# Group 3's reads: summed over d by a 0/1 matrix in two parts, then one float32 product with the outgoing weights

## What is computed

```python
x = layernorm(x + L0_attn(x))      # gated linear recurrence, 16 heads of 8
x = layernorm(x + x @ W[idx] + b[idx])   # one of 8 experts, chosen from logits and noise
x = layernorm(x + L1_attn(x))      # linear attention through a metric, 16 heads of 8
x = layernorm(x + L1_ffn(x))       # 128 -> 512 gated, 512 -> 512 gelu, twice, 512 -> 128
```

```python
k = sigmoid(x @ key_w.T + key_b)                 # [n, t, head, d]
upd = (1 - k)[..., :, None] * v[..., None, :]    # d x e per head
kv[t] = kv[t-1] * k[t] + upd[t]                  # a scan over t
h[e] = sum over d of q[d] * kv[d, e]
out = h @ out_w.T + out_b
```

## Time and profile before

| | us |
|---|---|
| median of 3 runs (193.44 to 194.26) | 193.96 |
| the profiled execution's own time | 193.92 |
| its span, first to last instruction | 192.1 |
| busy PE | 173.9 |
| busy DVE | 143.7 |
| busy ACT | 124.9 |
| busy POOL | 69.6 |

### The profile page before, as it was taken

How to read it: one execution, slowest core, us unless ns; L and a number is a source line. 1 busy time by engine, 2 the same in 40 slices (tenths; PEclk the granted TensorE clock), 3 DMA queues, 4 the chain that set the end, 5 groups by cost and what they waited for, 6 DMA issues and landing times. The chain is left out here.

```text
span 192.1 us, 2885 instructions
## 1 busy us (share of the span) xinstructions
PE 173.9 (91%) x949; PEld 138.1 (72%) x949; DVE 143.7 (75%) x371; ACT 124.9 (65%) x207; POOL 69.6 (36%) x65
## 2 busy tenths in 40 slices
PE   7779796999999999999999999999899999999930
PEld 7447483768977788888888899876678775586810
DVE  0799999999999997679979986668470774804461
ACT  3895915963838588648786560577887578975720
POOL 1020002640330662525172740442556336285320
PEclk9999999999999999999999999999999999999985
DMA  4879400210000001000000000000001000010102
GB/s 116 257 198 430 181 2 22 68 48 0 3 0 0 5 22 32 0 0 3 0 0 2 3 0 0 0 0 3 0 3 55 5 0 0 0 54 1 55 7 58
DMA packets 6705, 7.85 MB, mean 41 GB/s; under 512 B 544, under 2 KB 5664, under 8 KB 6432
## 3 DMA queue, kind: packets, MB, share of 16 engines
q1 hardware_dynamic: 6688, 7.63, 12.2%
HBM read 6.58 MB, written 1.05 MB: 40 GB/s over the span
## 5 line engine op out<-in xcount | busy, mean ns | idle before, releaser
L878 DVE TENSOR_TENSOR_SCAN state<-rep_bank,keep 128x256 f32<-128x256 f32 x62 | 38.6, 672 | 0.0
L347 POOL TENSOR_TENSOR rstd<-varied,power 128x4 f32<-128x4 f32 x15 | 15.9, 1063 | 57.0 <-DVE varied L937 57.0
L1335 PEld LDWEIGHTS y_bank<-attend_pack,read 128*128 128x128 f32 x256 | 31.4, 192 | 4.5 <-issue 2.6
L1335 PE MATMUL y_bank<-attend_pack,read 128*128 128x128 f32 x256 | 32.8, 276 | 0.7 <-DVE read L888 0.3
L585 ACT ACTIVATE hid_even_high<-c_bank,scales_pack 128x512 fp32r<-128x512 f32 x15 | 10.3, 689 | 17.9 <-PE c_bank L1430 17.9
L356 POOL TENSOR_TENSOR hid_odd_low<-hid,hid_odd_high 128x512 fp32r<-128x512 f32 x12 | 15.9, 1323 | 15.2 <-ACT hid L591 15.1
L591 ACT ACTIVATE hid<-c_bank,scales_pack 128x512 f32<-128x512 f32 x31 | 21.2, 684 | 0.0
L888 DVE TENSOR_TENSOR read<-state,query 128x512 f32<-128x512 f32 x28 | 20.8, 754 | 0.0
L1430 PE MATMUL c_bank<-hid_even_high,hidden_rounded 128*128 128x512 f32 x64 | 19.2, 411 | 0.5 <-ACT gate L574 0.5
L1430 PE MATMUL c_bank<-hid_odd_low,hidden_rounded 128*128 128x512 f32 x64 | 18.5, 398 | 0.5 <-DVE hid_odd_low L1033 0.5
L1430 PE MATMUL c_bank<-hid_even_low,hidden_rounded 128*128 128x512 f32 x64 | 18.7, 398 | 0.0
(11 more groups left out here) (189 smaller groups left out, 359.4 us busy)
## 6 DMA issues: line engine op xcount, KB each, us to landing
hidden_pack<-hidden SPq DMA_DIRECT2D x2, 1024.0 KB, 10.1
xt<-x_tok SPq DMA_DIRECT2D x4, 256.0 KB, 2.9
xT_lent<-x_chan SPq DMA_DIRECT2D x3, 256.0 KB, 4.6
mlp_pack<-mlp SPq DMA_DIRECT2D x1, 768.0 KB, 7.1
out<-xT_lent SPq DMA_DIRECT2D x3, 256.0 KB, 2.3
attend_pack<-attend SPq DMA_DIRECT2D x1, 640.0 KB, 4.2
metric_pack<-metric SPq DMA_DIRECT2D x1, 448.0 KB, 5.8
xT_lent<-x_chan SPq DMA_DIRECT2D x2, 128.0 KB, 2.5
```

The lines of the kernel that those rows point to most:

```text
L347: nc.gpsimd.tensor_tensor(rstd[n][:], varied[n][:], power[:], ALU.pow).then_inc(ln_rstd[n], 1)
L878: ins = nc.vector.tensor_tensor_scan(state[:, e % STATES, at], rep_bank[e % 2][:, at], keep[:, a * T + s * SEQ:a * T + (s + 1) * SEQ], 0.0 ...
L1335: ins = nc.tensor.matmul(y1_bank[:, tile(j)], read[:, e % READS, tile(j)], out_w_rep_sb[:, e, :], start=(e == 0 and j == 0), stop=False, s ...
```

## The change

For group 3 alone (`GATHERED = (3,)`) the eight `attend` calls go. In their place, for each `e`:

- `upper_read(3, e)` (ACT): copies `read` to `read_high`, rounded float32 (128x512, two buffers);
- `lower_read(3, e)` (DVE): `read - read_high` into `read_low`, which lies in the two buffers `dvalue_parts[0]` of the even groups' value steps;
- `gather(3, e)` (PE): two products of 512 columns, for the high and the low part, with a shifted window of a 0/1 matrix (`gather_r`) as weights. It sums over d and puts the 16 heads of index `e` on rows of their own in `y1_bank`.

After the last one `join(3)` (DVE) adds `direct` to `y1_bank` and writes `direct`, and `attend_joined(3)` (PE) multiplies that by `out_w` in four float32 products. `cast_gather` (ACT) rounds the matrix once; it comes in with the `metric` pack, which is 240 columns (120 KB) wider. The core of the diff:

```diff
+        gather_r = sb("gather_r", [P, GATHER], F32R)
+        read_high = sb("read_high", [P, 2, T], F32R)
+        read_low = dvalue_parts[0]
...
+            def upper_read(a, e):
+                act.wait_ge(*read_done(a, e))
+                if gathered(a, e) > 2:
+                    act.wait_ge(attended, HD * a + e - 1)
+                nc.scalar.copy(read_high[:, e % 2, :], read[:, e % READS, :]).then_inc(upper_done, 1)
...
+            def lower_read(a, e):
+                dve.wait_ge(upper_done, gathered(a, e))
+                if gathered(a, e) > 2:
+                    dve.wait_ge(attended, HD * a + e - 1)
+                nc.vector.tensor_tensor(read_low[e % 2][:], read[:, e % READS, :], read_high[:, e % 2, :].bitcast(F32),
+                                        ALU.subtract).then_inc(lower_done, 1)
+
+            def join(a):
+                dve.wait_ge(attended, HD * (a + 1))
+                dve.wait_ge(direct_ready, a + 1)
+                nc.vector.tensor_tensor(direct[a % 2][:], y1_bank[:], direct[a % 2][:], ALU.add).then_inc(joined, 1)
...
+            def gather(a, e):
+                if e == 0:
+                    pe.wait_ge(gather_cast, 1)
+                    pe.wait_ge(ln_sum[0], a)
+                    if a > 2:
+                        pe.wait_ge(ln_sum[3], a - 2)
+                at = (HD - 1 - e) * HEADS
+                pe.wait_ge(upper_done, gathered(a, e))
+                nc.tensor.matmul(y1_bank[:], gather_r[:, at:at + P], read_high[:, e % 2, :], start=(e == 0), stop=False)
+                pe.wait_ge(lower_done, gathered(a, e))
+                nc.tensor.matmul(y1_bank[:], gather_r[:, at:at + P], read_low[e % 2][:], start=False,
+                                 stop=(e == HD - 1)).then_inc(attended, 1)
+
+            def attend_joined(a):
+                pe.wait_ge(joined, GATHERED.index(a) + 1)
+                for j in range(NT):
+                    ins = nc.tensor.matmul(y1_bank[:, tile(j)], direct[a % 2][:, tile(j)], out_w_sb[:],
+                                           start=True, stop=True)
+                ins.then_inc(y1_ready, 1)
```

With this the lists of calls of PE, DVE, ACT and POOL are written anew nearly throughout, in all four groups; the other steps are the same ones, in another order. Of PE's list, for example:

```diff
+                hidden(0, 2, 3)
+                replicate(3, 4)
+                narrow(0)
                 transposes(1, 2)
-                hidden(0, 2, 2)
-                replicate(3, 2)
```

More of the change, by code:

```diff
@@ L755, in _ @@
             high_x3(3)
+            silu_table(3)
+            narrow_out(2)
             silu(3, 0)
-            narrow_out(2)
+            silu(3, 1)
             high_product(3, 0)
-            silu(3, 1)
             silu(3, 2)
@@ L1197, in _ @@
             norm_moments(2, 2)
+            norm_varied(2, 2)
+            join(3)
+            norm_out(2, 2)
+            low_gelu(1, 2, 2)
             norm_sum(0, 3)
-            norm_varied(2, 2)
+            low_gelu(1, 2, 3)
             norm_stats(0, 3)
             norm_moments(0, 3)
-            norm_out(2, 2)
             norm_varied(0, 3)
@@ L1650, in with_weights @@
-                hidden(0, 1, 2)
-                replicate(3, 0)
-                through_metric(1)
-                replicate(3, 1)
-                hidden(0, 1, 3)
-                metric_out(1)
                 attend(2, 6)
                 attend(2, 7)
+                attend_direct(2)
+                transposes(1, 1)
+                hidden(0, 1, 2)
+                heads_of(1)
+                hidden(0, 1, 3)
+                gram_of(1)
+                replicate(3, 2)
+                replicate(3, 3)
@@ L1658, in with_weights @@
+                mix(1)
                 hidden(0, 2, 0)
-                attend_direct(2)
+                through_metric(1)
                 hidden(0, 2, 1)
+                metric_out(1)
+                hidden(0, 2, 2)
+                hidden(0, 2, 3)
+                replicate(3, 4)
+                narrow(0)
                 transposes(1, 2)
-                hidden(0, 2, 2)
-                replicate(3, 2)
-                hidden(0, 2, 3)
-                replicate(3, 3)
+                replicate(3, 5)
@@ L1666, in with_weights @@
+                turn_back(0)
+                replicate(3, 6)
                 gate_of(1, 0)
+                transposes(2, 0)
                 up_of(1, 0)
-                narrow(0)
+                gate_of(1, 1)
+                routed(2)
                 up_of(1, 1)
-                transposes(2, 0)
-                replicate(3, 4)
-                gate_of(1, 1)
+                gate_of(1, 2)
+                gather(3, 0)
+                gate_of(1, 3)
                 up_of(1, 2)
-                turn_back(0)
@@ L1814 @@
         "blocks": blocks,
+        "gather": np.concatenate([np.zeros((P, P - HEADS)), blocks[:, ::HD], np.zeros((P, P - HEADS))], 1,
+                                 dtype=np.float32),
         "ident": np.eye(P, dtype=np.float32),
```

509 lines of the change are left out of this document (262 added, 247 removed).

## The result

| | before | after |
|---|---|---|
| median of 4 runs | 194.11 us | 197.05 us (196.73 to 197.3) |
| ratio, 95% interval | | 1.0163, 1.0127 to 1.02 |
| profiled execution, its span | 193.92, 192.1 | 196.82, 195.0 |

The account below looks back on a forecast made before the run. The start was taken as bound by DVE, PE as nearly gapless from the first gate to about 132 us. Saving -3.5, start -0.3, waits and 0.4 for POOL summed to +1.1: 195.0 us, range 192.0 to 197.4.

Parts of the forecast that it names:

- this mechanism: Main case: the new order's waits give back PE's saving and somewhat more, 193.5 to 196.3 us; chance 0.45.
- Saving: Group 3's sum on PE: eight gathers at 0.47 us instead of attends at 0.90, 3.5 us saved.
- The start: Up to the first gate product: DVE's list 0.5 us shorter, gate up to 0.5 us earlier, 0.3 taken.
- Item 2: After `hidden(0, 2, 3)` ends, at h: `replicate(3, 6)` needs a scan behind ACT and DVE; 1.3 us, bounds 0.3 and 2.
- Item 3: `product(1, 1)` behind `lower_read(3, 1)` and `norm_sum(1, 2)` moves `hidden(1, 1, 0)`: 1.0 us, bounds 0 and 1.5.
- the 0.4 which I had taken for the lock: Term for DVE steps held back by POOL at places without slack: 0.4 us added.
- Item 1: Blocks 2 and 3 of group 1 closer together, several waits between 58 and 92 us: 0.8, bounds 0 and 1.5.
- Item 4: `turn_back(1)` directly behind `narrow(1)` waits for ACT's `narrow_out`: 0.9 us, bounds 0.6 and 1.0.
- item 5: Group 2's gate stage: `norm_stats(1, 3)` makes `hidden(2, 1, 0)` late by 0.9; `metric_out(3)` waits 0.65; together 1.5 us.
- Item 6: Waits gone (0.31, 0.62, and 0.42 in group 3), 0.3 new before `hidden(3, 1, 0)`: net -1.0, bounds -1.35 and 0.
- DVE becomes the bound: Rival: POOL holds back subtractions and reads, group 3's sum 3 us later, 197 to 198; 0.12 together with the gathers' rival.
- the saving survives: Rival: items 1 to 3 and 5 near their lower bounds, sum -2.0, 191.9 us; chance 0.28.

Follow-up runs that it names:

- c_old_start: The changed kernel with the start of before (PE's list up to `attend(2, 2)`, DVE's up to `low_x3(0)`): 196.74 us, ratio 1.0112.
- i_best: The changed kernel's operations, lists of before up to 59 us, behind it some instructions of DVE, ACT and PE moved a few places: 192.76 us, ratio 0.9968.
- f_local: The changed kernel with four moves: `turn_back(1)`, `norm_stats(1, 3)` and `metric_out(3)` later, `product(1, 1)` ahead of `lower_read(3, 1)`: 200.04 us, ratio 1.0287.
- h_turn: The changed kernel with `turn_back(1)` behind `gate_of(2, 1)` instead of directly behind `narrow(1)`: 196.77 us, ratio 1.0151.
- a_before_order: The order of the kernel before on all engines, with only the change's operations put in: 201.63 us, ratio 1.0363.
- s_attend: The kernel before (attends, no gather) with instructions of PE, DVE, ACT and POOL moved by a few places: 195.62 us, ratio 1.011.
- s_gather: The changed kernel's operations, from the order of before, moved a few places in the manner of the attends' run, start included: 195.94 us, ratio 1.0127.

## Why the prediction was right, and which terms were wrong

The direction and the mechanism were right: PE's saving is real, and waits of the new order eat it up and more. The size was not: the sum came out at +1.1 and the kernel at +2.9. 197.05 us lies above the 193.5 to 196.3 that I gave to this mechanism; that it is inside the whole range, to 197.4, is owed to the case in which DVE is the bound, which did not come. To that extent it was luck. Term by term, with the table above:

- **Saving.** -3.5 forecast, -2.95 measured: a gather cost 0.47 as priced; five more changes from float32 to rounded products were left out.
- **The start.** This is the step that failed: "Up to 0.5 us earlier; I take 0.3", from counting DVE's instructions. The gate's low part came 1.05 later, and with `attend(2, 2)` still to do behind it. 1.9 us more of PE's time ahead of the gate is not work. A count of one engine's busy time holds only where nothing on it waits; between 50 and 59.5 us DVE waited for PE twice (0.22 and 0.17) and was held back beside POOL once (1.09 instead of 0.17), and the flag for PE's branch came late. By my own mark (the gate more than 1 us away from 58) the start was not fixed, and the table has it as the largest single term. That its delay is carried to the end in full is likely by c_old_start and i_best and not shown.
- **Item 2** was right in place and chain and somewhat small, 1.6 instead of 1.3: `replicate(3, 6)` started 4.45 us behind h (93.97 and 98.42), where I had 4.4.
- **Item 3** was right in place and small, 1.5 instead of 1.0, and its first step hardly counts: put ahead of `lower_read(3, 1)` and `norm_sum(1, 2)` in f_local, `product(1, 1)` waited for PE and started only 0.2 us sooner (102.76 against 102.70, with the rows ahead 0.27 later). What made the last two products late are `norm_stats`, `norm_moments` and `norm_varied(1, 2)`, which now stand between `product(1, 1)` and `product(1, 2)`: 2.04 us, from 103.36 to 105.40, where before nothing did. `norm_varied(1, 2)` took 0.75 of it beside POOL; that belongs to the 0.4 which I had taken for the lock.
- **Item 1**: 0.3 instead of 0.8.
- From `hidden(1, 1, 0)` to `narrow(1)`, for which I had nothing, the new order gained 0.4.
- **Item 4** and the first half of item 5, less the waits that went there (0.31 and 0.62): 0.9 forecast, 0.6 measured. The wait at `turn_back(1)` is there with 0.78 us, but h_turn showed that it covers another.
- **The second half of item 5**: 0.65 forecast, 1.5 measured. `metric_out(3)` waits 0.52 as forecast; that `transposes(3, 2)` would wait for `norm_out(2, 3)` right after, and run 0.4 slower tile by tile, I had not seen.
- **Item 6** in group 3: -0.1 forecast, -0.9 measured, since the gates had more lead.

With 1.9 for the start in the place of -0.3 the sum is +3.3, 197.2 us: the other errors cancel but for 0.4. Of the rivals, "DVE becomes the bound" gave nearly the right time by a wrong mechanism: n_no_lower takes the eight subtractions away and nothing changes. Its other sign, `lower_read` at a mean above 1.0 us, did not come either: they took 0.68, one of eight 1.37. Whether the saving survives in an order that is made for it, no run settles: i_best is 0.3% under before, at the edge of what the runs can tell.

The Trainium skill, SBUF — State Buffer, "SBUF: two separate sides", names beside instructions with two SBUF inputs those in a 2-port mode as taking the port pair that GpSimd shares. `norm_varied` has one input, and the trace has it held back all the same, 1.09 us beside POOL's read and 0.17 alone. That fits a 2-port mode; no row shows which mode it ran in.

## What to carry to other kernels

Price a change of order by the time that is not work up to the same place in both lists, not by adding up the waits that the profile prints: a wait often covers the next one, and taking it away alone gains nothing. When an operation becomes a chain over three engines, its place in the order must move with it; the same operations cost 7 us in the old order and gave back 1.9, beside attends, in the new one. Be careful with a start in which the matrix engine idles already: in s_attend a further wait there came with half the clock for 4 us and more.

## What the chip did that I had not expected

Once PE had stood for 2.4 to 3.0 us (a_before_order at 117.37, s_attend at 13.99), its granted clock read 0.50 for some 4 us or more, at full load: 1.2 instead of 2.4 GHz. The length of the wait alone doesn't tell: behind 1.18 us at 13.84 in s_gather the clock read 0.57 from 14 to 18 us, and behind 1.61 us at 31.46 in the changed kernel it stayed at 1.00. In c_old_start it fell to 0.59 from 24 to 28 us; the profile of a_before_order, which has the same start, kept 1.00 there. The kernel before has that start too, and its times spread from 191.7 to 196.6 us on these chips; whether the clock is the reason was not tried.
